# Sums over partitions of the weight scales: products with ones on TensorE in place of DRAM round trips, and GpSimd's bias additions at other places of the steps

## What is computed

```python
xn = _layernorm(x)
# attention: Q, K, V = xn @ Wq + bq, xn @ Wk + bk, xn @ Wv + bv   (512 -> 16 heads x 64)
scores = jnp.einsum('bhid,bhjd->bhij', Q, K)
columns = jnp.where(band, scores, 0.0)            # |i - j| <= 64
attn = jax.nn.softmax(columns, axis=-1)
attention = (attn @ V) @ Wo + bo
# network: s = xn @ Win + bin; h = relu(s * W1 + b1) (16 per feature); g = (h * W2).sum + b2
network = g @ Wout + bout
return x + attention + network
```

## Time and profile before

| | us |
|---|---|
| median of 3 runs | 2408.8 (2405.9 to 2411.8) |
| the profiled execution, its own time | 2410.0 |
| its span, from first to last instruction | 2408.3 |
| PE busy in the span | 2175.9 (90%) |
| DVE busy | 2020.5 (84%) |
| ACT busy | 1610.2 (67%) |
| POOL busy | 1368.4 (57%) |

### The profile page before, as it was taken

The page is one execution under the profiler, slowest core; times in us unless marked ns, Lnnn a source line. Parts: engine busy times, 40 slices in busy tenths (PEclk is TensorE's granted clock), DMA queues, the critical chain, the costliest instruction groups (busy, mean ns, idle before and its releaser), DMA issues.

```text
span 2408.3 us, 44273 instructions
## 1 busy us (share of the span) xinstructions
PE 2175.9 (90%) x14941; PEld 1290.1 (54%) x14941; DVE 2020.5 (84%) x5099; ACT 1610.2 (67%) x4344; POOL 1368.4 (57%) x1830
## 2 busy tenths in 40 slices
PE   4566766689999999999999999999999999999997
PEld 2233433355556565655556565655556565655664
DVE  2356666589998999889998999889998999889997
ACT  2355555567667776767767776767767776777765
POOL 3556655375556655565556655565556655565544
PEclk6778888899999999999999999999999999999999
DMA  3122111012111211112111211112111211111111
GB/s 101 32 57 58 40 40 62 24 45 84 32 36 29 82 54 32 36 45 84 32 36 32 81 52 32 36 45 84 34 34 32 82 51 32 36 45 49 36 32 44
DMA packets 75411, 115.04 MB, mean 48 GB/s; under 512 B 9884, under 2 KB 24628, under 8 KB 75188
## 3 DMA queue, kind: packets, MB, share of 16 engines
q1 hardware_dynamic: 74960, 112.20, 15.7%
q10 hardware_dynamic: 228, 0.02, 0.0%
HBM read 87.02 MB, written 25.18 MB: 47 GB/s over the span
## 4 chain that ended last, share of the span: by engine, by line
PE 64%; DVE 13%; POOL 10%; DMA 7%; ACT 3%; issue 2%; SPq 1%; ACTq 0%; DVEq 0%; POOLq 0%
PE ps L1248 29%; PE ps L1263 10%; PE ps L1313 9%; PE ps L1301 8%; POOL probs L427 5%; DVE probs L948 4%; PE ps L1234 4%; DMA top_kept<-top 3%; DVE acc L976 2%; PE ps L1291 2%; POOL acc L440 1%; DVE xn L994 1%; PE ps L1273 1%; PE ps L1204 1%; DMA top_all<-top_kept 1%
## 5 line engine op out<-in xcount | busy, mean ns | idle before, releaser
L1248 PE MATMUL ps<-xT_hi,w_split 128*128 128x512 f16 x3072 | 993.5, 385 | 139.1 <-DVE acc L976 106.1
L558 ACT ACTIVATE probs<-probs,neg_max 128x256 f32<-128x256 f32 x1024 | 506.0, 496 | 245.1 <-DVE neg_max L955 244.0
L427 POOL TENSOR_SCALAR probs<-probs,inv_l,neg_e 128x256 f32<-128x256 f32 x1024 | 565.0, 568 | 55.8 <-DVE neg_e L967 47.8
L1248 PE MATMUL ps<-xT_lo,w_split 128*128 128x512 f16 x1536 | 591.1, 385 | 0.0
L1248 PEld LDWEIGHTS ps<-xT_hi,w_split 128*128 128x128 f16 x3072 | 304.1, 99 | 503.8 <-DVE acc L976 117.0
L948 DVE CUSTOM_DVE_ANT_0 probs<-ps,mask,unit_s 128x256 f32<-128x256 f32 x1024 | 432.5, 477 | 16.4 <-PE ps L1234 16.2
L976 DVE SCALAR_TENSOR_TENSOR acc<-ps,unit_o,acc 128x512 f32<-128x512 f32 x512 | 369.1, 743 | 65.1 <-PE ps L1263 62.2
L612 ACT ACTIVATE pT_hi<-ps 128x512 f16<-128x512 f32 x512 | 276.5, 594 | 194.7 <-PE ps L1313 137.0
L1013 DVE TENSOR_TENSOR pT_lo<-ps,pT_hi 128x512 f16<-128x512 f32 x512 | 322.7, 678 | 18.2 <-ACT pT_hi L612 17.9
L1263 PE MATMUL ps<-wo_split,oT_hi 128*128 128x512 f16 x1024 | 309.2, 384 | 28.0 <-issue 9.8
L1301 PE MATMUL ps<-ident,probs 128*128 128x128 f32 x2048 | 263.9, 274 | 31.7 <-POOL probs L427 24.4
(11 more groups left out here) (120 smaller groups left out, 3471.0 us busy)
## 6 DMA issues: line engine op xcount, KB each, us to landing
w_split<-w_kept SPq DMA_DIRECT2D x168, 256.0 KB, 2.6
acc<-in_L_attn_x SPq DMA_DIRECT2D x14, 1024.0 KB, 5.6
out_x<-acc SPq DMA_DIRECT2D x14, 1024.0 KB, 4.5
wo_split<-wo_kept SPq DMA_DIRECT2D x56, 256.0 KB, 2.7
w_kept<-w_split SPq DMA_DIRECT2D x24, 256.0 KB, 4.5
acc<-in_L_attn_x SPq DMA_DIRECT2D x4, 512.0 KB, 5.6
w_raw<-in_L_attn_Wv SPq DMA_DIRECT2D x8, 256.0 KB, 4.7
w_raw<-in_L_attn_Wq SPq DMA_DIRECT2D x8, 256.0 KB, 4.4
```

The source lines that it names most:

```text
L427: pool.tensor_scalar(probs[:, h, t], probs[:, h, t], inv_l[:, c:c + 1], neg_e[:, c:c + 1], ALU.mult, ALU.add).then_inc(normed, 1)
L558: act.activation(probs[:, h, t], probs[:, h, t], ACT.Exp, bias=neg_max[:, c:c + 1], accum_out=row_sum[:, c:c + 1])
L1248: last = pe.matmul(dst[:], w[wp][:, i, c], xT[xp][:, c, half * LINE:half * LINE + LINE], start=(c == 0 and a == 0), stop=(c == KC - 1 and ...
```

## The change

- The sum over partitions becomes a matmul: `ones` (128 by 128, all 1.0) as weights times the columns of `top`; the result stands in all partitions of a PSUM bank at columns 32 and up. A second small matmul adds the squares of the pair's biases, so the floor from the largest bias becomes a sum of squares. All DMAs to and from `top_kept`, `tops_kept` and `bias_kept` and DVE's reductions are gone.
- In steps 1 to 7 PE computes the sums of V, Q, K of pair n+1 and of Wo of pair n-1 together, right after qk1 (`sum_step_tops`), after waiting for ACT's squares; in step 8 ahead of `project_out(3)`; in step 0 at its end. `project_out(3)` waits until DVE has read them, since it writes the same bank.
- DVE reads them (`read_tops`) after `mask_scores(3)` (in step 8 after `add_output(2)`), in step 0 at its end, and computes all scales and units of a step in one place, after `denominators(1)`.
- POOL takes one inverse root of four columns per step, after `split_qk(1)`.
- ACT's `output_top` moves behind `exps(1)`. In step 0 ACT's squares for pair 1 and their splits move to the end of the step, and on POOL the eight bias additions then stand behind the root and two weight splits.
- The biases are transposed on PE right at the start, and DVE's first instruction waits for them.
- In batches 1 to 7 `add_biases(0)` and `(1)` leave the step k = 0 ahead of `split_qk(3)`: (0) goes to that step's end, ahead of the split of Wo in step 8; in the step k = 1, (1) stands after `split_qk(2)`, (2) and (3) after `output_low(1)`.

```diff
 # SP
-                    if attend:
-                        share_output_top(k - 1)
-                    if split_next:
-                        share_tops(k + 1)
...
 # POOL
-                if attend and n <= PAIRS:
-                    inverse_root(slice(3, 4), o_top_ready, j + 1, o_root_ready)
...
                 if proj:
                     split_qk(1)
-                if split_next:
-                    inverse_root(slice(0, 3), top_ready, scales_of(n + 1, K_), root_ready)
+                if 0 < n <= PAIRS:
+                    inverse_root(tops_of_step(n), top_ready, scaled_in(n), root_ready)
+                if attend:
+                    normalise_weights(1)
+                if proj:
+                    split_qk(2)
                 if k == 1 and proj and b > 0:
-                    add_biases(2)
-                if attend:
-                    normalise_weights(1)
-                if proj:
-                    split_qk(2)
+                    add_biases(1)
+                if n == 0:
+                    inverse_root(tops_of_step(0), top_ready, scaled_in(0), root_ready)
                 if split_next:
                     split_low(n + 1, V_)
                     split_low(n + 1, Q_)
...
+                if attend:
+                    output_low(1)
+                if k == 0 and proj and b > 0:
+                    add_biases(0)
                 if k == 1 and proj and b > 0:
+                    add_biases(2)
                     add_biases(3)
...
 # DVE
+            def read_tops(cols, bank, done, count, ready):
+                dve.wait_ge(done, count)
+                dve.tensor_scalar(top_used[:, cols], ps[bank][:, TOP_COLUMN + cols.start:TOP_COLUMN + cols.stop],
+                                  W_TOP ** -2, (W_FLOOR / W_TOP) ** 2, ALU.mult, ALU.max).then_inc(ready, 1)
...
 # PE
+            def sum_tops(cols, bank, pair, done):
+                out = ps[bank][:, TOP_COLUMN + cols.start:TOP_COLUMN + cols.stop]
+                weights = cols.start < 3
+                last = pe.matmul(out, ones[:], top[:, cols], start=True, stop=not weights, skip_group_check=True)
+                if weights:
+                    biases = slice(cols.start, min(cols.stop, 3))
+                    last = pe.matmul(ps[bank][:, TOP_COLUMN + biases.start:TOP_COLUMN + biases.stop], ones[:],
+                                     bias_squared[:, biases, pair], start=False, stop=True, skip_group_check=True)
+                last.then_inc(done, 1)
+
+            def sum_step_tops(n, bank):
+                if n < PAIRS - 1:
+                    for i in (V_, Q_, K_):
+                        pe.wait_ge(w_top[i], n + 2)
+                if n > 0:
+                    pe.wait_ge(w_top[3], n)
+                sum_tops(tops_of_step(n), bank, n + 1, top_sum)
...
                     project_qk(1)
+                if 0 < n < PAIRS:
+                    masks_read(1)
+                    sum_step_tops(n, TOP_BANK)
```

More of the change, by code:

```diff
@@ L1220, in _ @@
                         last.then_inc(xT_done, 1)
+            pe.wait_ge(w_top[Q_], 1)
+            pe.wait_ge(w_top[K_], 1)
+            sum_tops(slice(1, 3), FIRST_TOP_BANK[1], 0, top_sum)
+            pe.wait_ge(w_top[4], 1)
+            pe.matmul(ps[FIRST_TOP_BANK[2]][:, TOP_COLUMN + 4:TOP_COLUMN + 5], ones[:], top[:, 4:5], start=True, stop=True) \
+                .then_inc(win_top_sum, 1)
             def step(n, b, k, proj=True, attend=True, out_proj=True, split=False, last=False, **_):
```

227 lines of the change are left out of this document (87 added, 140 removed).

## The result

The changed kernel takes 2303.5 us (median of 4 runs, 2302.8 to 2304.3) against 2407.3 for the kernel before beside it: ratio 0.957, 95% interval 0.955 to 0.958. That is 104 us less, where 91 were forecast. In a second session it came to 0.956 (0.954 to 0.958); one of its four runs took 2550.0 us at a lower granted clock (0.839 and not 0.98) and does not count in the ratio.

The account below looks back on a forecast made before the run. The prediction took waits in batch 0, where weights are scaled through DRAM round trips, as the bound. Its terms, -17.0 - 53 - 13.7 - 12.7 + 5.6 = -90.8 us, gave 2318 us, range 2294 to 2346.

Parts of the forecast that it names:

- The root as the step's mark: Steps 1 to 6: POOL's root of V, Q, K ends 8.77 us after qk_line(0); 51.0 us gained.
- The first part of the step: Steps 1 to 6, up to the end of qk_line(0): times kept from the old trace, no gain counted.
- Rival C: Steps 1 to 6: K's loads decide, TensorE's new wait is 9 us, six steps lose 22.8 us; 2351; chance 0.11.
- Step 0: Prologue and step 0: TensorE 24.6 us earlier, of which step 1 gets 17.0; bias additions on the path.
- The clock: Steps 1 to 6: 2.0 us gained from matmuls no longer run at the reduced clock after a shorter stop.
- Step 7: Batch 0, only Wo to scale: ACT's waits move behind its first two groups of exponentials; 13.7 us gained.
- Step 8: Wo's own round trip goes, less 3.5 us for scale operations and a pair of additions; 12.7 us gained.
- Batches 1 to 7: Moved bias additions: new 2.4 us wait at k = 2, 1.29 recovered at k = 1; 0.8 us longer each, +5.6.
- Rival B: Steps 2 to 6: TensorE's own earliness sets the step, some 4 us more each, 20 in all; 2298; chance 0.12.
- Rival D: Batch 0: TensorE stays at 1.2 GHz for the rest of each step after its stop, +140 us; 2459; chance 0.04.

Follow-up runs that it names:

- first_biases_early: The changed kernel with step 0's eight bias additions moved into POOL's idle times of step 0, ahead of the root: 2293.2 us, ratio 0.9533.
- waits_moved_alone: The kernel before with all its DRAM round trips, only the positions of the waits, Wo's square and Wo's root moved: 2384.5 us, ratio 0.9894.
- wait_filled: The changed kernel with 22 transposes of the identity in TensorE's wait for the squares in steps 1 to 6: 2304.2 us, ratio 0.9577.

## Why the prediction was right, and where it was not

The direction, the range and the likeliest mechanism held.

- **The root as the step's mark.** 8.77 us behind `qk_line(0)` was forecast, 9.03 measured in each of five steps. Of the missing 0.26, 0.18 is the root of four columns, 1.04 us and not 0.86. The two small matmuls, put at 0.2 us, took 0.36 to 0.56 for the one of the four columns alone; they were not on POOL's chain. The five steps of it carried 42 of the 91 us.
- **The first part of the step was taken as fixed.** This is the step of the sum that failed: "It can start when ACT has read qk0", with the time of that read copied from the kernel before. It had been made late by what the change removed: K's load landed later (some 10 us over five steps), at least in part for the column's write beside it, and Wo's square stood ahead of ACT's exponentials. Rival C had looked at the same wait with the wrong sign: it kept the long landings of the columns as a sign of slow loads, and did not ask what the writes themselves did to the loads.
- **Step 0.** -20.1 for -17. TensorE starts the last group, qk3, at 44.30 for 73.11, 28.8 us earlier where 24.6 were worked out, and of these 8.7 go to what stands ahead of the additions, for 7.6. V0 starts at 20.97 and not 22.3, since TensorE's work ahead of it ends at 17.97 and no longer at 19.62; the rest took 3.00 us for 2.7. V1 no longer waits. The bias additions were on the path, as first_biases_early shows.
- **The clock.** The 2.0 us for matmuls at the reduced clock stand for nothing that was found: the 2.3 us of the table lie where the clock is at its higher level in both kernels. That the two numbers are close is luck.
- **Step 7** came to 13.8 for 13.7. But waits_moved_alone shows that the place alone gives 3.3 of it; the forecast's argument, that both waits "move behind them", was enough only together with the short path.
- **Step 8** gives 3.6 us less. The forecast put it at a steady step plus 1.0 for the scale's operations. It left out the new wait: TensorE stood 2.62 us for DVE's read ahead of `project_out(3)`, since that read is queued behind DVE's addition 2, as these rows of step 8 show. No run takes this wait away, and 1.0 us stays open.

```profile
377.63 0.73 DVE L910 SCALAR_TENSOR_TENSOR acc<-ps,unit_o,acc 128x512 f32<-128x512 f32 x1
378.29 0.14 DVE L789 TENSOR_SCALAR top_used<-ps 128x1 f32<-128x1 f32 x1
...
378.48 0.60 PE L1227 MATMUL ps<-wo_split,oT_hi 128*128 128x512 f16 x2 [2.62 <-DVE top_used L789]
```

- **Batches 1 to 7.** The wait at k = 2 is there, 1.31 us on DVE and 2.10 on TensorE where 2.4 were worked out, and the 1.29 at k = 1 is gone. Forecast were 0.8 us a batch, measured 0.0 in three and 0.9 to 1.1 in two of the five whole batches of the trace. In the three the new wait costs the batch what the old one did; in the two TensorE's clock fell behind the stop, a cost that the sum did not have.
- **Rival B** asked for TensorE's earliness as the pace. Its time of 2298 was nearer, but its reason holds in part at most: with TensorE's product up to 1.5 us earlier (wait_filled) steps 4 and 5 gained 0.3 to 0.4 us each, not all of it.
- **Rival D**: after the stop of 3.51 us in step 4 the matmuls ran at the reduced level to about 218.7, then at the higher one: some 5 us, not the rest of the step.

## What to carry to other kernels

When a wait is removed, ask of every time that you copy from the old trace whether the removed work had made it late, its DMAs beside other DMAs above all. Do not credit a moved wait with the whole gain of a change that also shortens the path: moved alone it gave 26 of 104 us, since at its new place the long path was no longer hidden. When an edit is meant to make an engine later or earlier, read in its trace whether it did, before you conclude from a time that did not move. And where two chains start at the same event, look for the length of the second before you shorten the first.

## What the runs showed of the hardware

- A write of 128 pieces of 4 bytes, issued right behind a load of 256 KB on the same queue, goes with late loads: over 8 us in seven of twenty, in none of 50 without it. Ten of the twenty are of kernels that differ from the changed one by the writes alone, and three of these are late. It is not so in every step, and two such writes were no worse than one.
- The same stop of TensorE, 2.10 and 2.09 us in two batches, was followed by matmuls at the full rate in the one, and at the reduced rate for 3.4 us in the other (0.63 us and not 0.38 for one, in the rows above). That is the difference between the batches of 270.6 and 271.5 us above. The nine traces with this wait show 48 such stops in batches 2 to 7; behind 15 of them the clock falls. In the five traces without the wait it does not fall from batch 2 to the last 30 us. The windows behind the two stops are these (columns as in the earlier trace rows):

```profile
722.00:732.00 10.00, 9.31 (x51) 5.12 (x52) 9.54 (x32) 8.39 (x31) 7.30 (x12) 1.00 0.20 63
...
992.60:1002.60 10.00, 9.86 (x43) 4.72 (x44) 8.08 (x29) 8.03 (x29) 7.29 (x12) 0.83 0.05 7
```

The Trainium skill ("TensorE: Matmul & The Clock Gate", section "HAM oscillation — how this bites in real kernels") describes stops between bursts of matmuls, longer ones than these, as what costs a kernel its clock; here a stop of 2.1 us was followed by a fall in one batch (granted clock 0.83) and not in the other (1.00).
